# Summing gathered expert rows on VectorE beside the expert tiles, in place of diagonal products on TensorE

## What is computed

```python
logits = xs @ router_w.T
scores = sigmoid(logits)
_, idx = top_k(scores + bias[None, :], 4)
w = take_along_axis(scores, idx, axis=1)
w = w / (w.sum(-1, keepdims=True) + 1e-20)
# every expert e: y_e = (silu(xs @ wg_e) * (xs @ wu_e)) @ wd_e, hidden size 128
out = sum over the token's 4 experts of w * y_e  +  shared expert(xs)
x = x + out
```

## Time and profile before

| | us |
|---|---|
| runs shown (three) | 528.49, 530.16, 530.91; median 530.16 |
| span of the profiled execution | 527.9 |
| last instructions of TensorE and ScalarE begin | 522.10, 522.73 |
| first and last output DMA issued by SyncE | 522.4, 525.7 |
| gap of the median over that span | 2.3 |

### The profile page before, as it was taken

One profiled execution on the slowest core, in us unless ns is written; L12 is line 12 of the kernel. 1 busy time (PEld: TensorE's weight loads), 2 busy tenths in 40 slices (PEclk: granted clock), 3 DMA queues, 4 the chain that ended last, 5 costly groups with the idle time before them and its releaser, 6 DMA issues.

```text
span 527.9 us, 11484 instructions
## 1 busy us (share of the span) xinstructions
PE 489.7 (93%) x3222; PEld 431.4 (82%) x3222; DVE 405.2 (77%) x1040; ACT 283.8 (54%) x804; POOL 191.0 (36%) x232
## 2 busy tenths in 40 slices
PE   6899999999999999999999998979998999898985
PEld 6688899899898898898898898769875667776764
DVE  6689988988988988988988888787784753344465
ACT  2667656655655666666656564655425545522231
POOL 3417512312313313303303034426116666365640
PEclk9999999999999999999999999999989999999999
DMA  6441211210211211211100793299953456445544
GB/s 191 120 116 57 74 32 31 71 30 30 70 30 30 70 30 30 70 30 39 60 0 0 268 324 129 89 296 305 292 186 100 146 175 213 132 128 158 153 145 159
DMA packets 63269, 60.77 MB, mean 115 GB/s; under 512 B 5552, under 2 KB 60544, under 8 KB 63104
## 3 DMA queue, kind: packets, MB, share of 16 engines
q1 hardware_dynamic: 59024, 49.64, 31.0%
q0 software_dynamic: 3936, 10.55, 7.2%
q10 hardware_dynamic: 272, 0.13, 0.1%
HBM read 47.82 MB, written 20.87 MB: 130 GB/s over the span
## 4 chain that ended last, share of the span: by engine, by line
PE 63%; DVE 18%; issue 6%; ACT 6%; POOL 3%; DMA 1%; another core or an unknown queue 1%; DVEq 0%; SPq 0%; ACTq 0%; POOLq 0%
PE bank L998 12%; PE bank L1000 11%; PE bank L999 11%; PE bank L1239 11%; PE bank L1247 6%; DVE qk_lo L1759 4%; DVE rmax L1767 3%; DVE nmax L1771 3%; PE bank L1079 3%; ACT qk_hi L1497 2%; ACT prob L1505 2%; PE bank L1243 2%; DVE pT_lo L1792 1%; PE bank L1004 1%; PE bank L1373 1%
## 5 line engine op out<-in xcount | busy, mean ns | idle before, releaser
L1505 ACT ACTIVATE prob<-bank,nmax 128x256 f32<-128x256 f32 x128 | 59.5, 470 | 105.2 <-DVE nmax L1771 103.3
L711 POOL TENSOR_TENSOR w_lo<-st_c,w_hi 128x512 fp32r<-128x512 f32 x32 | 41.2, 1286 | 197.0 <-ACT w_hi L1468 197.0
L1239 PE MATMUL bank<-moe_w,xT 128*128 x252 | 66.0, 385 | 2.0 <-DVE xT L2067 1.8
L1759 DVE SCALAR_TENSOR_TENSOR qk_lo<-bank,b_col,qk_hi 128x512 fp32r<-128x512 f32 x64 | 47.8, 748 | 14.3 <-ACT qk_hi L1497 13.5
L998 PE MATMUL bank<-hT_hi,w_lo 128*128 128x512 f32 x128 | 52.7, 412 | 4.5 <-DVE qk_lo L1759 3.3
L1767 DVE TENSOR_REDUCE rmax<-bank 128x2 f32<-128x512 f32 x64 | 43.8, 685 | 13.8 <-PE bank L1000 13.3
L1239 PEld LDWEIGHTS bank<-moe_w,xT 128*128 128x128 f32 x252 | 45.2, 190 | 8.7 <-issue 2.9
L1000 PE MATMUL bank<-hT_hi,w_hi 128*128 128x512 f32 x128 | 50.6, 395 | 0.0
L999 PE MATMUL bank<-hT_lo,w_hi 128*128 128x512 f32 x128 | 50.5, 394 | 0.0
L1497 ACT ACTIVATE qk_hi<-bank,b_col 128x512 fp32r<-128x512 f32 x64 | 44.0, 687 | 8.6 <-PE bank L1000 7.2
L1785 DVE TENSOR_SCALAR prob<-prob,rinv 128x256 f32<-128x256 f32 x128 | 46.3, 403 | 2.3
(11 more groups left out here) (272 smaller groups left out, 1493.2 us busy)
## 6 DMA issues: line engine op xcount, KB each, us to landing
y_dram<-ysb SPq DMA_DIRECT2D x63, 128.0 KB
moe_w<-in_w_gate SPq DMA_DIRECT2D x8, 512.0 KB, 8.1
moe_w<-in_w_up SPq DMA_DIRECT2D x8, 512.0 KB, 7.8
moe_w<-in_w_down SPq DMA_DIRECT2D x4, 1024.0 KB, 9.0
st_c<-in_wq_codes SPq DMA_DIRECT2D x16, 128.0 KB
st_c<-in_wk_codes SPq DMA_DIRECT2D x16, 128.0 KB
st_c<-in_wv_codes SPq DMA_DIRECT2D x8, 256.0 KB
st_c<-in_wo_codes SPq DMA_DIRECT2D x8, 256.0 KB
```

Source lines behind the costliest of these rows:

```text
L1239: mm = pe.matmul(o, xT_of(kt), w, start=kt == 0, stop=kt == KT - 1)
L1505: ex = act.activation(prob[:, i % 4, qt, :], bS[i % 2][:, qt * S:(qt + 1) * S], ACT.Exp, bias=nmax[:, i % 2, qt:qt + 1], scale=SCALE, accu ...
L1759: dve.scalar_tensor_tensor(out=qk_lo[:, hp, m, n * HALF:(n + 1) * HALF], in0=src[:, :], scalar=b_col[:, bass.ds(g_h + m * H, 1)], in1=qk_h ...
```

## The change

- The diagonals, TensorE's products with them and ScalarE's three copies out are gone. VectorE does all 32 sums, in the order of the gathers; the first 28 stand one per step behind the products of tiles 35 to 62, four follow. Each waits for its own gather.
- ScalarE makes every copy into `ysb` from tile 31 on; VectorE makes none.
- SyncE's `AFTER` is 3: it confirms the store of tile n-3 after it has issued that of tile n.
- The output is issued by ScalarE, behind its last `ysb` copy, in four DMAs of two token tiles (256 KB) each.
- The gathers of the last k are in the order t = 0 to 7; each has a semaphore of its own; GpSimd reads the four limits of `y_done` once, ahead of the loop.

```diff
+SUM_FROM = ROWS + 3
@@ decoder_layer
-        out_order = (0, 1, 3, 2, 5, 4, 7, 6)
+        OUT_PAIRS = [slice(t, t + 2) for t in range(0, NT, 2)]
...
+        gather_order = [(t, k) for k in range(TOPK) for t in range(NT)]
+        summed = {t: gather_order.index((t, TOPK - 1)) + 1 for t in range(NT)}
@@ sync
-            AFTER = 1
+            AFTER = 3
...
-            for t in out_order:
-                if t in ON_TENSOR:
-                    sp.wait_ge(a_cmb, ON_TENSOR.index(t) + 1)
-                else:
-                    sp.wait_ge(v_cmb, combined[t])
-                sp.dma_start(out_rows[:, t, :], x_acc[:, t, :]).then_inc(d_out, 16)
-            sp.wait_ge(d_out, 16 * NT)
+            sp.wait_ge(d_out, 16 * len(OUT_PAIRS))
@@ gpsimd
-            pool.reg_load(at, need[0:1, :])
+            needed = [pool.value_load(need[0:1, k:k + 1], min_val=1, max_val=TILES) for k in range(TOPK)]
...
-                pool.wait_ge(y_done, pool.snap(at[k], min_val=1, max_val=TILES))
+                pool.wait_ge(y_done, needed[k])
@@ tensor
-            pe.wait_ge(v_diag, len(diag_order))
-            for t, k in tensor_order:
...
-                pe.matmul(into, diags[n // PER][:, n % PER, :], home(k)[:, t, :], start=k == 0, stop=False, skip_group_check=True)
-                if k == TOPK - 1:
...
-                    pe.matmul(into, ident[:, :], x_acc[:, t, :], start=False, stop=True, skip_group_check=True).then_inc(t_cmb, 1)
@@ scalar
-                if j == DEEP:
-                    wait(act, t_dn, SH + j - 2 + 1)
...
-                if j >= USED:
-                    n = j - 4
+                if j == DEEP or j > DEEP + 2:
+                    n = j - 2 if j == DEEP else j - 4
                     wait(act, t_dn, SH + n + 1)
-                    act.wait_ge(y_out, n)
                     wait(act, d_y[n % STEPS], (n // STEPS + 1) * 16)
                     act.copy(ysb[:, n % STEPS, :], bY[n % 2][:, 0:D]).then_inc(y_out, 1)
-            for t in ON_TENSOR:
-                act.wait_ge(t_cmb, ON_TENSOR.index(t) + 1)
-                act.copy(x_acc[:, t, :], bank[ON_TENSOR.index(t)][:, 0:D]).then_inc(a_cmb, 1)
+            for ts in OUT_PAIRS:
+                act.wait_ge(v_cmb, summed[ts.stop - 1])
+                act.dma_start(out_rows[:, ts, :], x_acc[:, ts, :]).then_inc(d_out, 16)
@@ vector
+            def weighted_sum(n):
+
+                t, k = gather_order[n]
+                if n == 0:
+                    dve.wait_ge(v_sh, NT)
+                    dve.wait_ge(d_xt, 16 * NT)
+                dve.wait_ge(d_yg[t][k], 16)
+                wait(dve, v_cmb, n - NT + 1)
+                dve.scalar_tensor_tensor(out=x_acc[:, t, :], in0=home(k)[:, t, :], scalar=factor[:, t, k:k + 1],
+                                         in1=x_acc[:, t, :], op0=ALU.mult, op1=ALU.add).then_inc(v_cmb, 1)
...
-            dve.wait_ge(y_out, DEEP - 1)
             for j in range(DEEP, USED):
-                if j == USED - len(diag_order):
-                    dve.wait_ge(d_xt, 16 * NT)
                 if j + 3 < USED:
                     tile_copy(j + 3, 0, ROWS)
-                if USED - len(diag_order) <= j:
-                    diagonals(j - USED + len(diag_order), 1)
                 product(j, j + SH)
-                if j > DEEP + 2:
-                    n = j - 4
-                    wait(dve, t_dn, SH + n + 1)
-                    wait(dve, d_y[n % STEPS], (n // STEPS + 1) * 16)
-                    dve.tensor_copy(ysb[:, n % STEPS, :], bY[n % 2][:, 0:D]).then_inc(y_out, 1)
...
+                if j >= SUM_FROM:
+                    weighted_sum(j - SUM_FROM)
+            for n in range(USED - SUM_FROM, len(gather_order)):
+                weighted_sum(n)
```

More of the change, by code:

```diff
@@ L453, in decoder_layer @@
         d_spare = sem("d_spare")
-        d_yg = [[sem(f"d_yg{t}_{i}") for i in range(TOPK - 1)] for t in range(NT)]
+        d_yg = [[sem(f"d_yg{t}_{k}") for k in range(TOPK)] for t in range(NT)]
         v_own = sem("v_own")
         v_cmb = sem("v_cmb")
-        v_diag, t_cmb, a_cmb = sem("v_diag"), sem("t_cmb"), sem("a_cmb")
         a_sh, a_row, v_slot, y_done = sem("a_sh"), sem("a_row"), sem("v_slot"), sem("y_done")
@@ L553, in decoder_layer @@
         R_SOURCE, R_TILE, R_TABLE = R_PLACED + PARTS, R_PLACED + PARTS + 1, R_PLACED + PARTS + 2
-        gather_order = [(t, k) for k in range(TOPK) for t in (range(NT) if k < TOPK - 1 else out_order)]
-        def place_of(k):
-            return max(0, k - 1)
+        gather_order = [(t, k) for k in range(TOPK) for t in range(NT)]
+        summed = {t: gather_order.index((t, TOPK - 1)) + 1 for t in range(NT)}
         FIRST_BESIDE = 32
@@ L883, in _ @@
                                         in_offset=bass.IndirectOffsetOnAxis(ap=dest[:, t:t + 1], axis=0)).then_inc(d_xt, 16)
-            at = [pool.alloc_register(f"need{k}") for k in range(TOPK)]
             pool.wait_ge(v_slot, S_NEED)
             apart(pool)
-            pool.reg_load(at, need[0:1, :])
+            needed = [pool.value_load(need[0:1, k:k + 1], min_val=1, max_val=TILES) for k in range(TOPK)]
             pool.wait_ge(d_xt, 16 * NT)
@@ L896, in _ @@
                 pool.wait_ge(t_gu, SH + min(USED, FIRST_BESIDE + n * 15 // 16))
-                pool.wait_ge(y_done, pool.snap(at[k], min_val=1, max_val=TILES))
+                pool.wait_ge(y_done, needed[k])
                 apart(pool)
                 pool.indirect_dma_start(out=home(k)[:, t, :], out_offset=None, in_=y_dram,
-                                        in_offset=bass.IndirectOffsetOnAxis(ap=y_slot[:, t, k:k + 1], axis=0)).then_inc(d_yg[t][place_of(k)], 16)
+                                        in_offset=bass.IndirectOffsetOnAxis(ap=y_slot[:, t, k:k + 1], axis=0)).then_inc(d_yg[t][k], 16)
         def ln_vector(dve, n, half, src):
@@ L1448, in _ @@
                     down(j - 4, expert(j - 4))
-            pe.wait_ge(v_diag, len(diag_order))
-            for t, k in tensor_order:
[L1451 to L1454, removed]
-                pe.matmul(into, diags[n // PER][:, n % PER, :], home(k)[:, t, :], start=k == 0, stop=False, skip_group_check=True)
-                if k == TOPK - 1:
-                    pe.wait_ge(d_xt, 16 * NT)
-                    pe.matmul(into, ident[:, :], x_acc[:, t, :], start=False, stop=True, skip_group_check=True).then_inc(t_cmb, 1)
         @block.scalar
@@ L1706, in _ @@
                     hidden_copy(j - 2, j - 2 + SH)
-                if j == DEEP:
-                    wait(act, t_dn, SH + j - 2 + 1)
-                    wait(act, d_y[(j - 2) % STEPS], ((j - 2) // STEPS + 1) * 16)
-                    act.copy(ysb[:, (j - 2) % STEPS, :], bY[j % 2][:, 0:D]).then_inc(y_out, 1)
-                if j >= USED:
-                    n = j - 4
+                if j == DEEP or j > DEEP + 2:
+                    n = j - 2 if j == DEEP else j - 4
                     wait(act, t_dn, SH + n + 1)
-                    act.wait_ge(y_out, n)
                     wait(act, d_y[n % STEPS], (n // STEPS + 1) * 16)
                     act.copy(ysb[:, n % STEPS, :], bY[n % 2][:, 0:D]).then_inc(y_out, 1)
-            for t in ON_TENSOR:
-                act.wait_ge(t_cmb, ON_TENSOR.index(t) + 1)
-                act.copy(x_acc[:, t, :], bank[ON_TENSOR.index(t)][:, 0:D]).then_inc(a_cmb, 1)
+            for ts in OUT_PAIRS:
+                act.wait_ge(v_cmb, summed[ts.stop - 1])
+                act.dma_start(out_rows[:, ts, :], x_acc[:, ts, :]).then_inc(d_out, 16)
         @block.vector
```

## The result

The changed kernel takes 525.6 us in the median of 20 runs (523.59 to 530.91), the kernel before, run beside it, 530.61 (528.27 to 532.67). The ratio is 0.992, 95% interval 0.990 to 0.994. Forecast were 523.9 us, range 521.5 to 527.0, against a base of 530.16: the direction and most of the size were right; the gain was 5.0 us instead of 6.3, and the time is 1.7 us above the forecast, as the kernel before also measured 0.45 us more than the base.

A forecast was written before the change was run, and what follows sets the result against it. TensorE was taken to bound the kernel up to 516.2 us, then an 11.3 us end with SyncE's late stores ahead of the output. Terms: -6.3 at the end, 0 in the tiles; 530.16 - 6.3 = 523.9 us, range 521.5 to 527.0.

The forecast's parts named there:

- rival 1: Old end: without a profile SyncE is not late, so the change brings only 4.2 us: 526.0; chance 0.15.
- The tail: From the last copy to the end of the span: about 5 us instead of 11.3.
- estimate by the data: Output at the end: data time of all parts decides, last part lands at 521.2, or 522.0 with stores in between.
- estimate by the issues: Output at the end: last issue plus a 1.8 us landing decides, last part lands at 520.3.
- The old tail: Kernel before, last expert tile to end: 11.3 us; SyncE's stores ahead of the output, 5.7 us, were the main term.
- ScalarE copies all rows: Tile stretch: 10.0 us more ScalarE work fits the 1.40 us steps; taken as 0, bounds -2 and +10.4.
- the bound of -2: Tile stretch: down product's release no longer passes through VectorE, saving its 0.4 us copy at each of five stops.
- Rival 2: Tile stretch gets shorter at the stops by up to 2 us: 521.9; chance 0.10.
- rival 4: Tile stretch: ScalarE becomes the bound, each of 28 steps grows by 0.372 us, 10.4 in all: 534.3; chance 0.05.
- Sums beside the tiles: 28 of 32 sums, 13.4 us, move into the steps at no cost; last sum ends near 514.9, ahead of the last copy.
- rival 3: Tile stretch: late gathers stop VectorE and delay products by 1 to 3 us: 525 to 527; chance 0.10.
- rival 5: Output at the end: moving it to another issuer saves only issue time, 1.9 us: 528.3; chance 0.05.

The follow-up runs named there:

- c_after: The changed kernel run again, unaltered, on a chip with stops: 527.32 us, ratio 0.992.
- c_before: The kernel before with only GpSimd's four limits read as in the changed kernel, on a chip with stops: 531.14 us, ratio 0.999.
- e4: The changed kernel with all 32 sums behind the last tile, on a chip with stops: 535.65 us, ratio 1.006.
- e1: The kernel before with AFTER = 3 and GpSimd's four limits read as in the changed kernel, no stops: 510.91 us, ratio 0.998.
- c_after_again: The changed kernel run again, unaltered, on a chip without stops: 507.44 us, ratio 0.990.
- e3: The changed kernel with its four output parts issued by SyncE behind its last store check, no stops: 508.38 us, ratio 0.993.
- e7: The changed kernel without the 16 gathers of the third and fourth kind, no stops: 506.93 us, ratio 0.988.
- v1: The changed kernel with the four output parts issued by GpSimd behind its last gather, with stops: 530.62 us, ratio 0.996.
- e5: The changed kernel with VectorE making the ysb copies of tiles 31 to 58, no stops: 506.89 us, ratio 0.991.
- e6: The changed kernel with VectorE making the ysb copies of tiles 31 to 58, run a second time, no stops: 507.45 us, ratio 0.990.
- e2: The changed kernel with AFTER = 1, no stops: 507.93 us, ratio 0.993.
- v2: The changed kernel with the first two output parts issued by SyncE between its last stores, two by ScalarE, no stops: 507.84 us, ratio 0.990.

## Why the prediction held, and where it did not

The gain came from where the prediction looked for it: the output no longer stands behind SyncE's waits. Luck had a part in the number. 525.6 lies just outside the band of the forecast (522.5 to 525.5) and nearer to the 526.0 of rival 1, whose mechanism fell; the range took it in because it was wide enough for the rivals.

*The tail.* Forecast 5.0 us from the last copy to the end, measured 4.85, and 5.28 without stops. The estimate by the data was the right one of the two bounds: a part lands 2.2 to 3.2 us behind its issue, not the 1.8 that stood in the estimate by the issues. From 519.5 us to its end c_after moves 1.31 MB, parts and last stores together, at 268 GB/s in the mean, where the output of before moved at 228. The four issues start 0.54 us apart, inside the bounds of 0.45 to 0.90 each. A part landing over 3 us behind its issue had been named as a sign of being wrong; 3.2 came, and the end was right all the same.

*The old tail.* This term was mis-sized by half a microsecond: 11.3 us in the one trace I had, 10.74 in c_before. Rival 1 (an old tail of 9.2 us where SyncE is not late) fell: SyncE waits for landings there too, 4.6 us in nine times against the 5.5 of the earlier trace rows, and its first output goes out 5.2 us behind the last copy. What the tail of the kernel before is without stops no trace shows. From SyncE's waits in c_before, from 516 us on:

```profile
SPq L661 <- DMA y_dram<-ysb: 4.6, 9, 0.9
...
SPq L689 <- ACT x_all L1718: 0.5, 1, 0.5
```

*ScalarE copies all rows.* I took 0 between -2 and +10.4, and said that no row shows how the queue behaves in the stops. Without stops 0 is right (46.30 us against 46.35 with the copies on VectorE). With stops the tiles end about 0.6 to 2.1 us later, as worked out from the tails and the medians above, and the cause stays open. For the copies speak the waits of the down product, 1.4 to 4.1 us where VectorE's copies had 0.2 to 0.4. Against them: TensorE's waits in all are no longer than in the first trace of before (6.7 to 7.0 us against 7.3), and the first trace of the changed kernel, without a fall of the clock, takes 52.3 us from gate/up of tile 31 to that of tile 62, as the kernel before did (52.2). The longer ones (54.0 to 54.7) have 6.8 us at the lower clock. No run with stops had the copies on VectorE, so neither the copies nor the later store checks nor chance can be told apart; e4 excludes the sums alone. Without stops, where the copies are free, the gain is no larger: 512.3 - 507.44 = 4.9 us. So part of what is missing from the 6.3 lies elsewhere: the old tail was 0.5 us shorter than in my one trace, and the new one is 0.4 longer without stops. What stops the engines on one chip and not on others stays open as well. The stops are also more than the five that I had worked out and based the bound of -2 on: seven of the steps from tile 32 to tile 62 take over 1.5 us, in the first traces of before and of after alike. Rival 2 (a shorter stretch) fell, and rival 4 (a step longer by 0.372 us in each of 28 tiles) too.

*Sums beside the tiles.* Right for the tiles: no stall of TensorE, and VectorE waited for no gather in the first trace, rival 3's margin of 1.0 us included. The end of the last sum was mis-sized: forecast 1.7 us ahead of the last copy, measured 1.0 ahead with stops and 0.7 behind without. With stops I had overlooked VectorE's own order: sum 31 stands behind the product of tile 62 and four other sums, and no gather holds it. From the first trace of after:

```profile
516.83 0.29 DVE L1907 TENSOR_TENSOR hid<-bank,sg 128x128 f32<-128x128 f32 x1
517.04 2.06 DVE L2126 SCALAR_TENSOR_TENSOR x_all<-yg,x_all 128x256 f32<-128x256 f32 x5
```

Without stops gather 31 is the reason. GpSimd has no pause between its gathers, and the sums make each longer. Gathers of e1 (sums not beside) and of c_after_again (sums beside), both without stops:

```profile
L898 POOL DMA_INDIRECT yg<-y_dram,y_slot x32: 945/949/1082, 454.1 to 494.8; - x32
```

```profile
L878 POOL DMA_INDIRECT yg<-y_dram,y_slot x32: 942/1098/1110, 454.3 to 496.8; - x32
L2126 DVE SCALAR_TENSOR_TENSOR x_all<-yg,x_all x32: 474/476/485, 458.7 to 500.0; 128x256 f32<-128x256 f32 x32
```

1.10 us against 0.95, while the sum keeps its 0.476. With stops the mean shows it: 0.95 us in e4, whose sums stand behind the tiles, 1.01 in c_after. The Trainium skill, "SBUF — State Buffer", Who interferes with whom, has the two contend; the rows agree that they do and that here GpSimd is the one that pays, but with 0.15 us a gather, not the full 0.48 of a sum that complete blocking would give. I had priced it as a bound and then used the adds of the earlier trace rows, which show only VectorE's side. The last two sums of c_after_again wait for it:

```profile
DVE x_all L2126 <- DMA yg<-y_dram,y_slot: 1.6, 2, 1.2
```

*Late checks.* `y_done` counted later cost nothing, as reckoned; the gain is 0.7 to 1.5 us.

*Only issue time saved* (rival 5, which the Trainium skill's "DMA: Bandwidth & Descriptors", Issuing engines are not separate DMA queues, taken alone would give): it fell. e3 moves the output back to SyncE with the same number of issues and loses 1.4 us of tail (0.9 in the medians).

*From span to time.* The 2.3 us that I kept between the span and the median were 1.75 us around the span, as the runs with both numbers show (510.55 against 508.8), and 0.5 of a trace that was faster than the median.

## What to carry to other kernels

An output should not stand in a queue behind waits that only confirm other transfers: read what the issuing engine waits for between the last result and the first output DMA. Work moved beside a loop was free here where the loop ran evenly; where it stops, these runs don't tell its price. A row of waits names who released an engine last; before it is called a cost, compare the total idle time and the granted clock of the same stretch. And one trace's tail or gap to the median is a sample: 11.3 and 10.7 us were the same kernel but for the four reads of GpSimd's limits.

## What the runs showed of the hardware

GpSimd's DRAIN at the end of the program ended 7.8 to 8.0 us after the start of its last DMA in thirteen of the fourteen traces, and 7.0 us after it in e7, which has half the gathers: 530.46 after 522.55 (v1), 522.1 after 514.16 (the changed kernel), 519.3 after 511.47 (before). In the kernel before it was hidden by 8 us. After the change it is done 2 to 3 us before SyncE with stops (522.1 against 524.7). Without stops it ends three traces, c_after_again, e5 and e6, by 0.1 to 0.5 us, while in e2, e3 and v2 SyncE comes last; from c_after_again:

```profile
L211 POOLq EVENT_SEMAPHORE  x2: 17/17/17, 504.8 to 504.9; - x2
L211 POOLq DRAIN  x1: 10974/10974/10974, 493.8 to 493.8; - x1
...
L211 SPq DRAIN  x1: 13/13/13, 504.7 to 504.7; - x1
```

SyncE is done at 504.7, GpSimd at 493.8 + 11.0 = 504.8, 8.0 us after the start of gather 31 (496.83). In e5 and e6, whose last gather starts at 497.1 and 497.2, GpSimd is done at 505.1 both times while SyncE had been done for 0.5 and 0.3 us. Whoever shortens this tail further will have to start the last gather earlier as well; with all gathers in place that was not tried.

TensorE's clock stood at its lower level in parts of the tile stretch of c_after, e4 and v1, at or behind stops of 1.4 to 2.8 us, and at no time in the tile stretch of the eight traces without stops.

The same kernel took 532.7 us on one chip and 512.3 to 512.5 on two others, with equal times up to the first expert tile (its gate and up end at 400.4 us both in c_after and in c_after_again) and the whole difference in the expert tiles.
